# Two loads of x per unit, issued by one engine or by two: a two-layer group-normalised convolution

## What is computed

```python
def _gn(v, G=4, eps=1e-5):
    g = v.reshape(B_, G, C_ // G, H_, W_)
    m = jnp.mean(g, axis=(2, 3, 4), keepdims=True)
    s = jnp.var(g, axis=(2, 3, 4), keepdims=True)
    return ((g - m) / jnp.sqrt(s + eps)).reshape(v.shape)

x = x + conv3x3(_gn(x), L0_weight) + L0_bias
x = x + conv3x3(_gn(x), L1_weight) + L1_bias
```

## Time and profile before

| | |
|---|---|
| median of 3 runs | 4281.35 us (4275.36 to 4285.82) |
| the profiled execution's own time | 4269.09 us |
| its span | 4267.1 us |
| TensorE busy | 3721.2 us (87%) |
| VectorE / ScalarE / GpSimd busy | 2030.0 / 1763.9 / 1357.5 us |
| moved by DMA | 1434.52 MB, mean 336 GB/s |
| queues q10 / q0 / q1 | 627.30 / 536.96 / 268.45 MB |

### The profile page before, as it was taken

The page is one execution under the profiler, slowest core; times in us unless marked ns, Lnnn a source line. Parts: engine busy times, 40 slices in busy tenths (PEclk is TensorE's granted clock), DMA queues, the critical chain, the costliest instruction groups (busy, mean ns, idle before and its releaser), DMA issues.

```text
span 4267.1 us, 89407 instructions
## 1 busy us (share of the span) xinstructions
PE 3721.2 (87%) x33232; PEld 1532.6 (36%) x33232; DVE 2030.0 (48%) x3110; ACT 1763.9 (41%) x1381; POOL 1357.5 (32%) x1797
## 2 busy tenths in 40 slices
PE   0087778988889998998889989999999999999999
PEld 0032223333333333343333333344565333333333
DVE  7966666555564444445556344434445222322222
ACT  0032223333334554533333555544443555555554
POOL 0011111111113444521111445441111555555555
PEclk9999999999999999999999999999999999999999
DMA  9899999999999999999999999999999999999998
GB/s 352 358 350 372 380 370 362 330 381 373 376 368 301 356 357 352 321 331 375 368 371 346 311 354 360 347 281 362 354 360 330 288 294 289 280 275 288 289 279 255
DMA packets 367072, 1434.52 MB, mean 336 GB/s; under 512 B 49888, under 2 KB 50016, under 8 KB 334176
## 3 DMA queue, kind: packets, MB, share of 16 engines
q10 hardware_dynamic: 176736, 627.30, 48.4%
q0 software_dynamic: 153344, 536.96, 33.4%
q1 hardware_dynamic: 36864, 268.45, 17.1%
HBM read 895.64 MB, written 536.87 MB: 336 GB/s over the span
## 4 chain that ended last, share of the span: by engine, by line
PE 56%; DMA 30%; DVE 5%; issue 4%; POOL 2%; ACT 2%; ACTq 1%; DVEq 0%; POOLq 0%; SPq 0%
PE conv L633 55%; DMA x_tile<-x_dram 20%; DMA x_tile<-mid_dram 9%; DVE bn_x L682 2%; POOL x_tile L407 2%; DMA stat_tile<-x_dram 1%; DVE out_tile L709 1%; ACT x_tile L509 1%; ACTq L480 1%; DVE bn_mid L692 1%; ACT out_tile L466 0%; ACTq L493 0%; DVE mv_mid L720 0%; DVEq L682 0%; POOL out_dram L387 0%
## 5 line engine op out<-in xcount | busy, mean ns | idle before, releaser
L633 PE MATMUL conv<-x_tile,wts 64*64 64x512 f32 x32832 | 3703.6, 600 | 333.1 <-issue 139.8
L633 PEld LDWEIGHTS conv<-x_tile,wts 64*64 64x64 f32 x32832 | 1512.3, 134 | 2505.3 <-issue 2432.9
L466 ACT ACTIVATE out_tile<-conv,bias 128x1024 f32<-128x1024 f32 x688 | 729.1, 1111 | 1387.8 <-PE conv L633 1387.8
L692 DVE BATCH_NORM_STATS2 bn_mid<-out_tile 128x512 f32 (+1 forms) x1376 | 850.0, 680 | 920.2 <-ACT out_tile L466 920.2
L709 DVE TENSOR_SCALAR out_tile<-conv,bias 128x1024 f32<-128x1024 f32 x340 | 436.3, 1283 | 1271.1 <-PE conv L633 1271.1
L373 POOL DMA_DIRECT2D mid_dram<-out_tile x680 | 344.7, 508 | 1751.9 <-ACT out_tile L466 1677.6
L509 ACT ACTIVATE x_tile<-x_tile 16x2048 f32<-16x2048 f32 x340 | 648.6, 1908 | 290.5 <-DMA x_tile<-mid_dram 248.8
L387 POOL DMA_DIRECT2D out_dram<-out_tile x680 | 349.8, 516 | 920.9 <-DVE out_tile L709 720.9
L682 DVE BATCH_NORM_STATS2 bn_x<-stat_tile 128x512 f32 (+1 forms) x1024 | 629.4, 678 | 25.1 <-DMA stat_tile<-x_dram 24.6
L407 POOL COPY x_tile<-x_tile 16x2048 f32<-16x2048 f32 x340 | 639.7, 1881 | 0.6
L471 ACT ACTIVATE out_tile<-conv,bias 128x1024 f32<-128x1024 f32 x344 | 383.5, 1115 | 615.7 <-PE conv L633 608.7
(11 more groups left out here) (62 smaller groups left out, 115.6 us busy)
## 6 DMA issues: line engine op xcount, KB each, us to landing
x_tile<-x_dram ACTq DMA_DIRECT2D x680, 512.0 KB, 11.7
stat_tile<-x_dram SPq DMA_DIRECT2D x256, 1024.0 KB, 9.9
out_dram<-out_tile POOLq DMA_DIRECT2D x680, 384.0 KB, 7.7
mid_dram<-out_tile POOLq DMA_DIRECT2D x672, 384.0 KB, 8.9
x_tile<-mid_dram ACTq DMA_DIRECT2D x340, 640.0 KB, 6.4
x_tile<-mid_dram ACTq DMA_DIRECT2D x344, 128.0 KB, 8.3
mid_dram<-out_tile POOLq DMA_DIRECT2D x8, 416.0 KB, 9.4
x_tile<-x_dram ACTq DMA_DIRECT2D x8, 256.0 KB
```

Source lines behind the costliest of these rows:

```text
L466: last = act.activation(out_tile[0:parts, slot, i], conv[0:parts, bank, i], ACT.Identity, bias=bias0[0:parts, win.parity, int(unit.last), ...
L633: last = nc.tensor.matmul(to, weights, x_tile[HALF * half:HALF * (half + 1), slot, middle, c + kw:c + kw + BANK], start=(kw == 0), stop=(k ...
L692: last = dve.bn_stats(bn_mid[0:parts, unit.win.pair % 2, i, bass.ds(unit.n * 2 + h, 1), :] .rearrange("p a b -> p (a b)"), out_tile[0:part ...
```

## The change

Of a layer-0 unit's two loads, band 0 stays with ScalarE and band 1 goes to SyncE. In each step SyncE first does what it did for the statistics, then waits until the unit's convolution is done, and issues band 1 of the unit four later. It does so where that unit belongs to layer 0 and isn't the last one. At the start it issues band 1 of units 0 to 3 ahead of the first statistics tiles. In the last steps of a layer-1 window it also waits for the halo copy out of the slot, as ScalarE already does.

```diff
+        slots_free = sem("slots_free")
...
+        def load_band(queue, unit, band):
+
+            win, slot = unit.win, unit.slot
+            rows = x[win.image:win.image + 2, :, bass.ds(row_in(unit, band), ROWS_IN), :]
+            queue.dma_start(x_tile[:, slot, band, 1:SIDE + 1],
+                            rows.rearrange("n c r w -> (n c) r w")).then_inc(x_loaded[slot], 16)
+
...
                         load_stat(win.x_pair, k * win.x_each + (win.x_first + s + win.x_each), s,
                                   k * win.x_each + (x_tiles_before(win) + s + 1))
+                    following = unit.after(RING)
+                    if following is not None and following.win.layer == 0 and not following.last:
+                        sp.wait_ge(conv_done, unit.count + 1)
+                        sp.sem_inc(slots_free)
+                        if win.layer == 1 and not unit.last:
+                            sp.wait_ge(first_halo, halos_through(unit.after(1)))
+                        load_band(sp, following, 1)
 
                 in_order(sp, win, step)
 
+            for b in range(RING):
+                load_band(sp, Unit(WINDOWS[0], b), 1)
             for s in range(STAT_SLOTS):
                 load_stat(0, s, s)
...
                 if win.layer == 0 and not unit.last:
-                    for band in range(BANDS):
-                        rows = x[win.image:win.image + 2, :, bass.ds(row_in(unit, band), ROWS_IN), :]
-                        act.dma_start(x_tile[:, slot, band, 1:SIDE + 1],
-                                      rows.rearrange("n c r w -> (n c) r w")) \
-                            .then_inc(x_loaded[slot], 16)
+                    load_band(act, unit, 0)
                     return
```

## The result

The changed kernel takes 4390.28 us (median of 4 runs, 4375.28 to 4409.4) against 4283.59 (4 runs, 4275.36 to 4288.98): ratio 1.0264, 95% interval 1.0225 to 1.0303. It is slower by 107 us. The forecast was 4271, no measurable change, with 4312 as the upper end of the range.

A forecast was written before the change was run, and what follows sets the result against it. Windows 0, 1 and 3 were held to wait for x, with q10 backlogged and DMA engines full. Start -6, window 0 +10, windows 1 and 3 -14 gave -10 us: 4259 against the profiled 4269, so 4271 as median; range 4222 to 4312.

The forecast's parts named there:

- The bound: Windows 0, 1 and 3 wait for x: its queue q10 is always backlogged and the DMA engines are full.
- the untouched windows: Windows 2, 4, 6 and 7 load from `mid` by code the change doesn't touch; layer-1 windows were to keep their length.
- C: Rival: no effect, the same bytes on the same engines, gain and loss cancel; 4275 to 4281 us, chance 0.16.
- rival B: Slower: band 1 stands behind statistics in its queue and stores' cover is spent where not needed; +38 us, 4319, chance 0.22.
- Two x and a store, r: Time of one packet from each of two x queues and a store queue on one DMA engine: 0.532 us taken, 0.468 to 0.579 considered.
- two x packets alone: Two x packets on one DMA engine with no store: taken as twice x alone, 0.532 us.
- My own formula: Whole kernel's change in us: -10 + 1024 x (r - 0.532), r being the time of two x packets and a store.
- the rounds: One packet per active queue on one DMA engine, summed over units: window 0 +10 us, windows 1 and 3 together -14 us.
- The start: Band 1 loads ahead of the first statistics tile lose 2.0 to 5.5 us, 11.6 come back from VectorE's waits; -6 us taken.
- The windows' heads: Statistics loads behind SyncE's wait: VectorE may wait some 10 us at unit 5 of windows 1 and 3; counted nothing, uncovered 20.

The follow-up runs named there:

- stat_pool_two: Changed kernel with the windows' statistics tiles issued by GpSimd behind its stores: 4482.42 us, 1.0494 of the kernel before; the same without the split 4455.19 us.
- row_pitch: No computation, loads and stores in 16 phases: distance between groups of 8 rows varied, then units by one queue and two; window 1's mix 2% longer when split.
- dma_mixes: DMAs alone in 16 phases of different queue mixes, no computation: the changed kernel's mix took 133 us, the mix before 128.
- contig_two: Changed kernel with each x load's 128 rows taken from one run in HBM: 4130.64 us, 0.9676 of the kernel before; the same without the split 4127.76.
- sbuf_side: Loads alone in 14 phases, varied on the SBUF side: contiguous rows into 64 partitions 203 GB/s, 8 of every 9 rows 233.
- cut_loads: Loads and stores in 12 phases, no computation, a band's load cut into pieces of every second or fourth row and partition: cut in 4 on one queue 201 GB/s.

## Why the prediction was wrong

**What was right.** The bound (q10 backlogged, DMA engines full, windows 0, 1 and 3), that the untouched windows keep their length, that C's plain count of bytes is not enough, and the side to fear, rival B, which stood at 0.22 with 4319 us. In window 0 band 0 lands sooner and band 1 no sooner (24.1 us), as foreseen; in window 1 it is the other way round. Of B's two parts the runs support the first, band 1 in the queue of the statistics: out of it the split costs 0.6% (stat_pool_two), and without statistics nothing (row_pitch). The second, x without a store's cover, fits window 0, where there is more such time, and not window 1, where there is less. B's size, +38 us, was too small as well.

**The step that failed** is "Two x and a store, r": I took 0.532 us, on the thought that two x packets cost no more beside each other than alone and that the store is hidden. Measured in dma_mixes it is 0.601, above my upper bound of 0.579, and two x packets alone take 8192 x 16/238 = 0.551 (238 GB/s inside that phase), above 0.532. Nor is r one number: by the count in the changed kernel's trace it is 12288 x 16/327 = 0.601 in window 1 and 12288 x 16/364 = 0.540 in window 3, and there the units behind the head lose nothing. My own formula, -10 + 1024 x 0.069, then gives +61 us. By the rounds the sign of the whole hung on r being above 0.542, and I took a value 2% below that from a row that didn't show the mix.

**The start** was to give 6 us and gave none: +67.

**The windows' heads** I priced at nothing, looking only at VectorE's wait. Behind the four tiles stands band 1, and TensorE waited 17.2 us for it. Against 9.7 us lost by two units at the same place before (9.5 + 10.6 less twice 5.2) the unit of 25.3 us loses 20.1, about 10 us more: +77. All heads together, units 5 to 12 of windows 0, 1 and 3, lose 35 us, of which the formula with r = 0.601 has 8.4; the rest is 17 us more than these 10. I had named what is queued behind SyncE's wait, but not what is queued in the DMA queue behind what SyncE issues.

**What stays open** is about 30 of the 107 us, 17 of which lie in the heads, and how the rest is spread. The rounds with r = 0.601 give +0.44 us a unit in window 0 and +0.31 in windows 1 and 3; measured are +0.94, +0.74 and +0.09, and behind the heads (units 13 to 64) +0.75, +0.63 and -0.02. So the formula with the measured r is too small for windows 0 and 1 and wrong for window 3; that it comes to more than half of the loss is in part luck. Without waits the mixes lose only 0.31 (133 against 128 us over 16 units) and 0.12 (109 against 107). So the larger part needs both the dear reads (contig_two loses nothing) and something that these phases lack. The likely thing is the units' own rhythm, in which stores come only after a convolution, but I didn't test the rhythm by itself. TensorE's clock adds something that I haven't separated: granted 0.93 of full speed in 250 to 700 us before and 0.88 after, with TensorE busy for 342 and 320 of the 450 us; 48 matmuls take 5.9 us before and 6.2 after. Why window 3 is spared in two executions of the changed kernel isn't known; its bands land together (12.4 and 13.3 us in 2000 to 2350), those of window 1 don't (18.7 and 11.1).

## What to carry to other kernels

A backlogged queue is not by itself a reason to split it: here the split cost 2.6%. First read what each kind of packet costs in each mix of queues; where one kind is dear alone and cheap beside another (x at 246 GB/s alone, x and a store at 419), the split changes who meets whom, and that can cost more than the wait. Don't put an urgent load into a queue that also holds bulk prefetches issued in bursts (one stood behind four tiles here, and TensorE waited 17.2 us). And when the sum turns on one unseen price, measure or bound it wide before believing a forecast of no change.

## What the runs showed of the hardware

A load of 16 groups of 8 rows of 4 KB into 128 partitions runs at 228 to 267 GB/s by itself at any distance between groups that was tried (36 KB to 4 MB + 32 KB; row_pitch and sbuf_side), at 207 with two pairs of images on two queues (dma_mixes), and the same packets from one run of HBM at 388 (row_pitch, sbuf_side). 4 MB gave 237 to 267 GB/s and 4 MB + 4 KB gave 233, so the added 4 KB didn't help. Contiguous loads into 64 partitions give 203 GB/s with packets of 4 KB and of 8 KB (sbuf_side). A cut that makes each piece take every fourth row and partition, with the pieces issued by two engines, gives 282 GB/s where the uncut load on one queue gives 253, at a DMA share of 0.99 and 1.00; pieces of every second row and partition give 277 on one queue (cut_loads). While a store is beside it (402.2 to 404 us of the kernel before) a packet of the slow load takes 159 ns in the median and 160 in the mean, where alone (446.3 to 448.8 us) it takes 267 in the median and 271 in the mean.

Why the load is slow isn't shown. That much of the limit lies on the side that writes SBUF is my guess, from the loads into 64 partitions (203 against 388 GB/s) and the cut (277 and 282 against 253); but the cut changes the order of the reads too, and the 207 GB/s speak for HBM.
